# Attention: scores of two heads at a time, and projection in six-matmul runs in front of them

## The reference, cut to what matters

```
# per batch b: x (512, 1024), ctx (512, 256); LN = layer norm
q  = LN(x)                                  # 16 heads of 64
k = v = ctx                                 # 4 groups of 64, each for 4 heads
probs = softmax(q_h @ k_g.T / 8)            # (512, 512) per head
out = concat_h(probs @ v_g)                 # (512, 1024)
x = x + out @ Wc.T + bc
x = x + ffn(LN(x))                          # router, top 8 of 32 experts
```

## Time and profile before

| | us |
|---|---|
| median of 3 runs (9379.66 to 9392.39) | 9384.93 |
| the profiled execution | 9424.62 |
| its span | 9422.8 |
| TensorE busy, of the span | 9114.1 |
| VectorE busy | 6400.5 |
| ScalarE busy | 4227.1 |
| GpSimd busy | 5243.0 |

### The profile page before, as it was taken

How to read it: one execution, slowest core, us unless ns; L and a number is a source line. 1 busy time by engine, 2 the same in 40 slices (tenths; PEclk the granted TensorE clock), 3 DMA queues, 4 the chain that set the end, 5 groups by cost and what they waited for, 6 DMA issues and landing times.

```text
span 9422.8 us, 173720 instructions
## 1 busy us (share of the span) xinstructions
PE 9114.1 (97%) x46640; PEld 7509.9 (80%) x46641; DVE 6400.5 (68%) x9216; ACT 4227.1 (45%) x7011; POOL 5243.0 (56%) x4825
## 2 busy tenths in 40 slices
PE   8999999999969999999999999999999999999999
PEld 5777777777747888888888888888888888888888
DVE  5666666666646767777666667677777667766676
ACT  6666666666633433333333333333333333333333
POOL 2444444444445656666556566565666566656564
PEclk9999999999979999999999999999999999999999
DMA  2222212112114545555454455455555455544554
GB/s 96 59 57 59 61 55 63 58 55 64 57 60 105 117 106 115 116 124 128 109 111 110 111 132 114 108 113 114 117 116 127 105 121 114 116 107 111 127 113 82
DMA packets 787085, 926.16 MB, mean 98 GB/s; under 512 B 403473, under 2 KB 600081, under 8 KB 786578
## 3 DMA queue, kind: packets, MB, share of 16 engines
q0 software_dynamic: 209920, 604.72, 29.8%
q1 hardware_dynamic: 430866, 165.82, 7.1%
q10 hardware_dynamic: 145920, 151.01, 5.0%
HBM read 1076.32 MB, written 376.45 MB: 154 GB/s over the span
## 4 chain that ended last, share of the span: by engine, by line
PE 63%; DVE 3%; issue 2%; ACTq 1%; another core or an unknown queue 0%; ACT 0%; POOL 0%; DMA 0%; DVEq 0%; SPq 0%; POOLq 0%
PE bank L1581 41%; PE bank L1604 22%; DVE gu_lo L1495 1%; DVE xT L1484 1%; DVE xT_lo L1489 0%; ACTq L1383 0%; DVE h L1507 0%; DVE h_hi L1510 0%; DVE h_lo L1512 0%; ACTq L1375 0%; POOL xg L1329 0%; ACT xT_hi L1396 0%; DVE d_lo L1500 0%; DVE rows_out L1519 0%
## 5 line engine op out<-in xcount | busy, mean ns | idle before, releaser
L1329 POOL DMA_INDIRECT xg<-xn_rows,gather_row x2304 | 2970.1, 1289 | 1882.5 <-PE bank L1581 1271.4
L1581 PE MATMUL bank<-xT_hi,gu_hi 128*128 128x512 f32 (+2 forms) x6912 | 2557.1, 370 | 118.2 <-DVE xT_lo L1489 107.7
L1581 PE MATMUL bank<-xT_lo,gu_hi 128*128 128x512 f32 (+2 forms) x6912 | 2544.6, 368 | 0.0
L1581 PE MATMUL bank<-xT_hi,gu_lo 128*128 128x512 f32 (+2 forms) x6912 | 2544.5, 368 | 0.0
L1414 ACT ACTIVATE gated<-bank 128x512 f32<-128x512 f32 x432 | 258.6, 599 | 3047.0 <-PE bank L1581 2826.9
L1581 PEld LDWEIGHTS bank<-xT_hi,gu_hi 128*128 128x128 f32 x6912 | 1300.4, 188 | 302.1 <-issue 95.7
L1341 POOL DMA_INDIRECT out_rows<-rows_out,entry_now x576 | 1101.7, 1913 | 682.3 <-DVE rows_out L1519 399.0
L1581 PEld LDWEIGHTS bank<-xT_lo,gu_hi 128*128 128x128 f32 x6912 | 1300.7, 188 | 158.2
L1581 PEld LDWEIGHTS bank<-xT_hi,gu_lo 128*128 128x128 f32 x6912 | 1300.1, 188 | 158.8
L1604 PE MATMUL bank<-d_hi,h_hi 128*128 128x512 f32 x3162 | 1247.1, 394 | 53.7 <-DVE h_lo L1512 41.8
L1484 DVE STREAM_TRANSPOSE xT<-xg 128x512 f32<-128x512 f32 x1152 | 1284.1, 1156 | 13.6 <-DMA xg<-xn_rows,gather_row 13.6
(11 more groups left out here) (160 smaller groups left out, 12733.6 us busy)
## 6 DMA issues: line engine op xcount, KB each, us to landing
d_raw<-in_L_ffn_down_proj ACTq DMA_DIRECT2D x144, 1536.0 KB
gu_raw<-in_L_ffn_gate_proj ACTq DMA_DIRECT2D x145, 1024.0 KB
gu_raw<-in_L_ffn_up_proj ACTq DMA_DIRECT2D x145, 1024.0 KB
gu_raw<-in_L_ffn_gate_proj ACTq DMA_DIRECT2D x145, 512.0 KB
gu_raw<-in_L_ffn_up_proj ACTq DMA_DIRECT2D x145, 512.0 KB
xg<-xn_rows,gather_row POOLq DMA_INDIRECT x2304
x_t<-in_x SPq DMA_DIRECT2D x64, 512.0 KB, 4.8
inv_wide<-inverse_sums SPq DMA_DIRECT2D x512, 64.0 KB
```

Source lines behind the costliest of these rows:

```text
L1329: pool.indirect_dma_start(out=xg[:, m, :], out_offset=None, in_=quarter_rows, in_offset=bass.IndirectOffsetOnAxis(ap=gather_row[:, m:m + 1 ...
L1581: last = nc.tensor.matmul(bank[:, 0:cols], w[:, c, n, j * P:(j + 1) * P], v[:, c, 0:cols], start=(c == 0 and w is gu_hi and v is xT_hi), s ...
```

## The change

AHEAD stays 3, but TensorE issues scores at odd h only, for heads h + 3 and h + 4 in a row, still in front of `transpose_probs`. Each of the two banks has a semaphore of its own for finished scores. `PROJECT` now has an entry at each even h and none at odd h: half 0 of the tile before at h = 0, 2, 4, 6 and half 1 at h = 8 to 14, two chunks (six matmuls) each. In an even step the projection now comes last but for the queries, so behind `transpose_xn2` and `router`; the next thing in the queue is the pair of scores. At odd h `transpose_queries` comes right behind the scores and in front of `transpose_probs`. The tail's first projection takes chunk 0 too, and four heads of scores are issued in front of the first tile in place of three.

```
--- before.py
+++ after.py
@@ -183,7 +183,7 @@
             v_ready, kt_done = sem("v_ready"), sem("kt_done")
             khi_copied, klo_copied = sem("khi_copied"), sem("klo_copied")
 
-            scores_done, max_ready, exp_ready = sem("scores_done"), sem("max_ready"), sem("exp_ready")
+            scores_done, max_ready, exp_ready = [sem(f"scores_done{n}") for n in range(2)], sem("max_ready"), sem("exp_ready")
             inverse_turned = sem("inverse_turned")
             inverse_stored, inverse_wide, onorm_ready = sem("inverse_stored"), sem("inverse_wide"), sem("onorm_ready")
             inverse_ready = sem("inverse_ready")
@@ -218,9 +218,7 @@
             DVE_HEAD = 1
             VALUE_CHUNKS = {1: (0, 1), 3: (2, 3)}
 
-            PROJECT = {0: (1, 0, 1, 2), 1: (1, 0, 2, 3), 2: (1, 0, 3, 4), 3: (1, 0, 4, 5), 4: (1, 0, 5, 6), 7: (1, 0, 6, 8),
-                       8: (1, 1, 0, 2), 9: (1, 1, 2, 3), 10: (1, 1, 3, 4), 11: (1, 1, 4, 5), 12: (1, 1, 5, 6), 13: (1, 1, 6, 7),
-                       14: (1, 1, 7, 8), 15: (0, 0, 0, 1)}
+            PROJECT = {h: (1, h // GROUP_HEADS // 2, h % 8, h % 8 + 2) for h in range(0, H, 2)}
             NEXT_STATS, NEXT_FACTORS, NEXT_NORM, NEXT_SPLIT, NEXT_QUERIES, NEXT_BIAS = (1, 2), 2, 6, 7, (10, 11, 12, 13), 8
             RESIDUAL, STATS2 = (8, 15), (11, 15)
             FACTORS2, NORM2, TRANSPOSE2, ROUTER, CHOOSE, MARK, TOP_EXP = 0, 3, (4, 5), 6, 7, (11, 13), 8
@@ -588,7 +586,7 @@
                                       ).then_inc(klo_copied, 1)
 
                 def maximum(i, h):
-                    dve.wait_ge(scores_done, H * i + h + 1)
+                    dve.wait_ge(scores_done[h % 2], H // 2 * i + h // 2 + 1)
                     dve.tensor_reduce(neg_max[:, h:h + 1], S_BANK[h % 2][:, :], AX.X, ALU.max, negate=True
                                       ).then_inc(max_ready, 1)
 
@@ -794,10 +792,11 @@
                     if h % 4 == 0 and s == 0:
                         pe.wait_ge(khi_copied, 2 * (G * b + g + 1))
                         pe.wait_ge(klo_copied, 2 * (G * b + g + 1))
-                    wait(pe, exp_ready, H * i + h - 1)
-                    nc.tensor.matmul(S_BANK[h % 2][:, :], qT[s % 2][:, h, :], kT[:, g, :], start=True, stop=False)
-                    nc.tensor.matmul(S_BANK[h % 2][:, :], qT[s % 2][:, h, :], kT_swapped[:, g, :], start=False, stop=True
-                                     ).then_inc(scores_done, 1)
+                    for r in range(2):
+                        wait(pe, exp_ready, H * i + h + r - 1)
+                        nc.tensor.matmul(S_BANK[r][:, :], qT[s % 2][:, h + r, :], kT[:, g, :], start=True, stop=False)
+                        nc.tensor.matmul(S_BANK[r][:, :], qT[s % 2][:, h + r, :], kT_swapped[:, g, :], start=False, stop=True
+                                         ).then_inc(scores_done[r], 1)
 
                 def transpose_probs(i, h):
                     pe.wait_ge(exp_ready, H * i + h + 1)
@@ -886,13 +885,30 @@
                     nc.tensor.matmul(turned(j, 0)[:, E:2 * E], ones_bf[:, :], chosen[:, :], start=True, stop=True
                                      ).then_inc(rank_done, 1)
 
+                def scores_ahead(t, h):
+
+                    if h + AHEAD < H:
+                        scores(t.b, t.s, t.i, h + AHEAD)
+                    elif t.next:
+                        scores(t.next_b, t.next_s, t.i + 1, h + AHEAD - H)
+
+                def project_at(t, h):
+
+                    if h in PROJECT and (t.back1 or not PROJECT[h][0]):
+                        back, n, c0, c1 = PROJECT[h]
+                        project(t.i - back, n, list(range(c0, c1)))
+
+                def queries_at(t, h):
+
+                    if h in NEXT_QUERIES and t.next:
+                        transpose_queries(t.i + 1, NEXT_QUERIES.index(h))
+
                 def tile(t):
                     i = t.i
                     for h in range(H):
-                        if h + AHEAD < H:
-                            scores(t.b, t.s, i, h + AHEAD)
-                        elif t.next:
-                            scores(t.next_b, t.next_s, i + 1, h + AHEAD - H)
+                        if h % 2:
+                            scores_ahead(t, h)
+                            queries_at(t, h)
                         transpose_probs(i, h)
                         if h % GROUP_HEADS in VALUE_CHUNKS:
                             if h >= GROUP_HEADS:
@@ -904,26 +920,24 @@
                             transpose_keys(b, g)
                         if h == RANKS and t.back3:
                             ranks(i - 3)
-                        if h in PROJECT and (t.back1 or not PROJECT[h][0]):
-                            back, n, c0, c1 = PROJECT[h]
-                            project(i - back, n, list(range(c0, c1)))
                         if h in TRANSPOSE2 and t.back2:
                             transpose_xn2(i - 2, TRANSPOSE2.index(h))
                         if h == ROUTER and t.back2:
                             router(i - 2)
-                        if h in NEXT_QUERIES and t.next:
-                            transpose_queries(i + 1, NEXT_QUERIES.index(h))
+                        if h % 2 == 0:
+                            project_at(t, h)
+                            queries_at(t, h)
 
                 transpose_keys(0, 0)
                 transpose_keys(0, 1)
                 for n in range(4):
                     transpose_queries(0, n)
-                for h in range(AHEAD):
+                for h in (0, 2):
                     scores(0, 0, 0, h)
                 all_tiles(pe, tile)
                 values(B - 1, SC - 1, LAST, G - 1, range(TC))
                 ranks(LAST - 2)
-                project(LAST, 0, list(range(1, 4)))
+                project(LAST, 0, list(range(0, 4)))
                 project(LAST, 1, list(range(0, 4)))
                 for n in range(NH):
                     project(LAST, n, [4, 5])
```

## The result

The changed kernel takes 9661.5 us (median of 4 runs, 9655.6 to 9665.6) where the kernel before takes 9387.2 (median of 4 runs on the same chip): 1.0292 of it, 95% interval 1.0275 to 1.031. The forecast was 9543, with a range from 9455 to 9605. The sign was right and the loss, 274 us, was 1.7 times the 158 that I had worked out.

A forecast was written before the change was run, and what follows sets the result against it. TensorE's full queue alone was taken to set an ordinary tile's time. Per-tile terms of +2.0 us (32 ordinary), +2.75 (16 first) and +3.15 (16 last) gave 158 us on 9384.9: 9543 us, range 9455 to 9605.

The forecast's parts named there:

- The rival by which a quarter of the tile was slack: Whole attention tile: little to merge, and waits vanish in slack that a busy share hides; 9385 us, chance 4%.
- X0 with S7 in front of it: First xn2 transpose (step 4), with head 7's scores (step 3): TensorE arrives before ScalarE's normalised row and waits 1.30 us.
- Router: Router matmuls, step 6: TensorE arrives before ScalarE's second copy of the transposed xn2 is ready and waits 0.54 us.
- The second score of step 9: Scores of head 13: wait for exp of head 11, behind ScalarE's query split and copy; 0.3 us.
- The saving at the changes between fp32 and fp32r: TensorE's queue: fewer entries into fp32r work, less dearer transposes behind values; 0.4 us saved a tile, bounds 0 and 0.8.
- Queries: Second and fourth query transposes wait for ScalarE's copies of those before; with head 15's scores 0.3 us together.
- Last and first tiles: A batch's last tile +3.15 us (key and value copies, queries), its first +2.75 us (longer chain, waits behind it).
- the second score of each pair: Odd steps: head h+4's scores wait for exp of h+2; six projection matmuls just cover it, except 0.3 us at step 9.
- S15: Scores of head 15, second of step 11, behind exp of head 13: a wait of 0.07 us.
- rival 4: Clock falls once more per batch, behind the first tile's first xn2 transpose: +16 to +27, +45 more; 9560 to 9615, 15%.
- An S5 wait above 5 us: Sign at the loop's turn: head 5's scores, reached earlier, wait about 2.8 us longer for VectorE, some 5.3 us.
- X0's wait takes nearly all of the longer S5 wait back: First tile: the first xn2 transpose's 2.63 us wait absorbs most of head 5's longer wait; chain end moves some 0.6 us.

The follow-up runs named there:

- e2: The changed kernel with GpSimd's add of the bias at its step 11 instead of 8: 9540 us, 1.0153 of the kernel before.
- e7: The changed kernel with GpSimd's bias add over 8 of 1024 columns, at its old step 8: 9499 us in a single run.
- e3: The changed kernel with projection in front of xn2 transposes and router again, and the bias add at step 11: 9453 us, 1.0057 of the kernel before.
- e8: e3 with the second score of step 1 behind probs transposes, values and ranks in a batch's first tile: 9423 us, 1.0025 of the kernel before.
- e9: e8 with three projection matmuls moved from the next tile's step 0 to behind the values at each batch's end: 1.0025 of the kernel before.
- e1: The changed kernel with projection in front of the xn2 transposes and router again in steps 4, 5 and 6: 9591 us, 1.0206 of the kernel before.

## Why the forecast was wrong

**What bounds the kernel:** right. TensorE's queue was balanced within a fraction of a us, and each new wait came out as time. The rival by which a quarter of the tile was slack fell: in e2 the waits of an ordinary tile, 2.45 us from start to start, make it 2.0 us longer, and the rest is what the order saves. The Trainium skill (Perfetto Trace Analysis, Identifying the Most-Contended Engine) takes the busy share of weight loads for the better measure of headroom. Here it is 29.1 of 41.5 us, and yet no wait went into slack; in this kernel the measurement decides against that reading, and the distance from start to start was the measure that held.

**The terms of an ordinary tile, one by one,** from start to start. X0 with S7 in front of it: forecast 1.30 us, measured 1.37 in e2. Router: forecast 0.54, measured 0.47. The second score of step 9: forecast 0.3, measured 0.26. The saving at the changes between fp32 and fp32r: forecast 0.4; the tiles of the changed kernel and of e2, less all their waits, are both 39.06 us against 39.51, so 0.45. (The count behind it was not exact: a score behind a query transpose pays for an entry too, 0.31 against 0.23 us, so 21 entries become 10 and not 17 become 8; T directly behind the values takes 0.41 us against 0.35, as taken.) These four were of the right size. Queries: forecast 0.3, and no query transpose of an ordinary tile waits in e2 or e7. That e2's tile is nevertheless the forecast 41.5 is luck: a second score of step 13 is 0.35 us late in it, by the moved add; in e7 it is not, and the tile is 41.2.

**Last and first tiles** were forecast at +5.9 us a batch and are +5.3 in e2 (92.9 against 87.5), but by other terms, so that is luck too. The waits of the last tile's queries (0.75 and 0.4 more) are not in e2. Some 1.7 us of T0 at the turn were not in the sum, nor what the lower clock adds, 1.3 us a batch more than before. In e7, with less work on GpSimd, the two tiles are 2.9 us longer.

**The step that failed** is in the paragraph on the second score of each pair: "By the same intervals 0.12, 0.13, and 0.07 for S15: 0.3 us together (bounds 0 and 0.6)". S15 idles 1.69 us, 1.97 from start to start. The same intervals are ScalarE's: the copy behind T10, exp, then the score. They take VectorE's maximum of head 13 as long done, and no sentence gives a term to `oT_lo`, which VectorE does just before that maximum, nor to GpSimd. In the ordinary tile of the rows of before, `oT_lo` of step 9 took 1.5 us where it takes 0.42 at other steps, and I had not asked why. By name, the kernel before, 400 to 2600 us (least, median and most ns):

```profile
L621 DVE TENSOR_TENSOR oT_lo<-o_norm,oT_hi x212: 424/426/2695, 403.7 to 2597.0; 128x256 fp32r<-128x256 f32 x106
```

The most is six times the median. It was the same collision with GpSimd's add, cut short by its timing: in the kernel before, the add begins 1.2 us in front of `oT_lo` in the second and the fourth tile of a batch, and in the third it is past or nearly past when `oT_lo` begins. The change moves VectorE's step 9 and GpSimd's step 8 against each other, so that `oT_lo` starts before the add and is held through all of it, 3.33 us. The upper bound should have been its own length and a whole add. The sign that the prediction had named for this step did show: a tile of 43.2 us and more, above 42.5, means that the second scores wait more than was counted.

The Trainium skill has a rule that I did not weigh (SBUF — State Buffer, section Who interferes with whom): a VectorE instruction with two inputs in SBUF contends with a GpSimd instruction that reads SBUF, and the contention is an exclusive lock. The traces agree: the subtraction has two SBUF inputs and ends 0.3 us behind the add's end, while maxima, which read PSUM, take their usual 0.69 us beside the same add (in e2 and e3). The Trainium skill's same section also has it that the order of issue decides who is blocked. Here the record of `oT_lo` begins 0.64 us in front of the add's and it is held all the same; that is open.

**The clock** (rival 4): it fell, but mostly elsewhere than I had said. It fell behind the S15 wait, in 26 of 30 ordinary tiles, at 1.5 us each. In e2, without that wait, it fell in none. An estimate for the stage from the traces, half of the time that TensorE works at the lower level: 19 us in the kernel before, 83 in the changed kernel, 37 in e2 and e3, 19 in e8. So of the 274 us some 64 are the clock. Of the 137 us by which attention in the profiled run of e2 is shorter than in the changed kernel, some 46 are the clock and most of the rest the waits (64 us of score and query waits in 2200, some 80 in the stage). And in e2 the 143 us contain some 18 of clock that the sum of 158 had not. (The rival's own price had a slip: 3 us at half speed lose 1.5 us, not 1.7.)

**The loop's turn:** I had kept the 0.74 us of the kernel before. TensorE's queue runs empty behind the values now, and 1.6 to 2.1 us show. An S5 wait above 5 us, which was to be seen, is nowhere in the changed kernel (3.2 at most); in e2, T0's 1.7 and S5's 4.0 to 4.6 come near it together. Before, 0.8 us of projection stood behind them. Wrong was also that X0's wait takes nearly all of the longer S5 wait back: e8, which only lets TensorE work in front of that wait, is 0.3% faster than e3. A part of that, some 17 of 30 us, is the clock, which falls for less time behind the shorter wait.

**What is not shown:** whether any form of this beats the kernel before. The best, e8, is 0.25% slower. Its ordinary tile is 0.4 us longer: from start to start the second scores of steps 3, 9 and 13 are 0.24, 0.26 and 0.35 us late, and the order gives 0.45 back. The last of the three hangs on the moved add, so a step for the add that holds nothing with a wait behind it would give some 0.35 us a tile, about 20 of e8's 24 us by this estimate. No run tried one.

## What to carry to other kernels

When an engine's queue is full, merging work in it pays only what the seams cost (here 0.45 us of 39.5), and every instruction that moves forward loses the cover that stood in front of it: count, for each, the distance to its latest input before and after. Ask of every instruction that is longer at one place than elsewhere what holds it, because a change of order can make a hidden collision of two other engines the longest link. An off-path collision of this kind is cheap to look for: move the other engine's instruction to another step, and see what it holds there.

## What the runs showed that I had not expected

A VectorE subtraction of 0.42 us took 3.33 beside a GpSimd add of 2.40 whose record begins 0.64 us later; with the same add over 8 columns it took 0.46, and a GpSimd scatter of 1.0 us over the same moment did not hold it. In e3 the moved add holds another instruction with two SBUF inputs (2.30 us for `hot`, else 0.42), and a maximum, its exp and the second score of step 13 stand behind it, which idles 0.08 us and is 0.35 late from start to start:

```profile
1011.50 2.30 DVE L656 TENSOR_TENSOR hot<-top_f,iota_e 128x256 f32<-128x256 f32 x1
...
1014.44 0.68 DVE L590 TENSOR_REDUCE neg_max<-bank 128x1 f32<-128x512 f32 x1
```

```profile
1011.14 2.37 POOL L397 TENSOR_TENSOR x_t<-x_t,bias_row 128x1024 f32<-128x1024 f32 x1
```

In e7, where `hot` takes 0.41 us, that score comes without a wait.

TensorE stood 1.4 to 2.1 us at the turn of the loop when its queue was empty there, VectorE 2.8 to 5.7 depending on the order of the kernel; three matmuls queued in front hide some 0.6 of TensorE's (1.75 on average in e8, 1.12 in e9). The granted clock fell in 26 of 30 ordinary tiles of the changed kernel and in 10 of 30 of e1, each time behind S15's wait of 1.7 us; in e2, where no wait of an ordinary tile is longer than 0.9 us, it fell in none.
